# Local attention and the second projection of a vision-transformer block in one loop (Trainium2)

## The reference

```python
qkv = roll(xt @ w1.T + b1, (-2, -2))            # windows of 16 positions, 8 heads of 32
wei = einsum('bhijpe,bhijqe->bhijpq', Q, K) / scale + pos_emb[rel]   # masks in the last row and column
out = einsum('bhijpq,bhijqe->bhijpe', softmax(wei), V)
h = out.reshape(b, ht * wd, c) @ w2.T + b2      # the "hidden" product
qkv = layernorm(h) @ qkv_w + qkv_b              # q, k, v of the full attention
```

## Time and profile before

| | us |
|---|---|
| median of 3 runs | 6507.51 (6507.16 to 6508.6) |
| profiled execution | 6517.03, its span 6515.1 |
| window_attention and project_qkv, first matmul to last store | 105 to 1444.5 |
| PE busy over the span | 5921.2 (91%) |
| DVE, ACT, POOL busy | 4386.3 (67%), 3220.7 (49%), 4313.3 (66%) |

### The profile page before, as it was taken

The page is one execution under the profiler, slowest core; times in us unless marked ns, Lnnn a source line. Parts: engine busy times, 40 slices in busy tenths (PEclk is TensorE's granted clock), DMA queues, the critical chain, the costliest instruction groups (busy, mean ns, idle before and its releaser), DMA issues. The chain is left out here.

```text
span 6515.1 us, 122324 instructions
## 1 busy us (share of the span) xinstructions
PE 5921.2 (91%) x37810; PEld 3470.1 (53%) x37810; DVE 4386.3 (67%) x8624; ACT 3220.7 (49%) x6628; POOL 4313.3 (66%) x1449
## 2 busy tenths in 40 slices
PE   2777767769999999999999999999999999987899
PEld 2666645545555555555555555555555555533566
DVE  2666633337777778777777777777777777737540
ACT  1444421113666666666666666666666666651222
POOL 0222222234888888888888888888888888874453
PEclk9999989987999999999999999999999999997899
DMA  1111134442100110110110011011011000014432
GB/s 40 41 41 45 43 110 158 158 165 58 34 26 24 34 34 16 35 47 17 34 31 26 24 35 35 21 43 34 16 34 31 25 16 23 14 38 126 121 94 40
DMA packets 216264, 323.65 MB, mean 50 GB/s; under 512 B 42228, under 2 KB 181078, under 8 KB 212694
## 3 DMA queue, kind: packets, MB, share of 16 engines
q1 hardware_dynamic: 200670, 295.36, 15.8%
q0 software_dynamic: 12432, 19.38, 1.5%
q10 hardware_dynamic: 2664, 2.62, 0.2%
HBM read 179.54 MB, written 137.35 MB: 49 GB/s over the span
## 5 line engine op out<-in xcount | busy, mean ns | idle before, releaser
L1193 DVE TENSOR_REDUCE tops<-ps_m 128x1 f32<-128x448 f32 (+1 forms) x5600 | 3120.2, 618 | 906.6 <-PE ps_m L1096 856.5
L1169 ACT ACTIVATE prob<-ps_s 128x448 f32<-128x448 f32 (+1 forms) x5600 | 2613.6, 548 | 1749.4 <-PE ps_s L1032 1707.5
L1002 POOL TENSOR_TENSOR tile_sum<-prob 128x1792 f32<-128x1792 f32 x448 | 1803.5, 4026 | 658.3 <-ACT prob L1169 658.0
L1032 PE MATMUL ps_s<-queries,keys 97*128 97x448 f32 (+1 forms) x5600 | 2196.9, 397 | 15.3 <-ACT prob L1169 7.5
L1096 PE MATMUL ps_m<-keys,queries 96*128 96x448 f32 (+1 forms) x5600 | 2090.5, 380 | 35.7 <-DMA keys<-k_parts 20.6
L1002 POOL TENSOR_TENSOR tile_sum<-tile_sum,prob 128x1792 f32<-128x1792 f32 x448 | 1808.0, 4036 | 31.8
L1032 PEld LDWEIGHTS ps_s<-queries,keys 97*128 97x128 f32 (+1 forms) x5600 | 1041.4, 187 | 1156.3 <-ACT prob L1169 662.2
L1048 PE MATMUL ps_o<-prob,values 128*32 128x448 f32 x11200 | 1342.3, 551 | 3.0 <-ACT prob L1169 1.2
L1096 PEld LDWEIGHTS ps_m<-keys,queries 96*128 96x128 f32 (+1 forms) x5600 | 1061.3, 190 | 240.5 <-DVE tops L1193 84.5
L257 POOL TENSOR_TENSOR logit<-logit,top 112x896 f32<-112x896 f32 x112 | 188.6, 1684 | 559.5 <-DVE top L374 559.5
L1048 PEld LDWEIGHTS ps_o<-prob,values 128*32 128x32 f32 x11200 | 226.5, 108 | 379.5 <-issue 245.0
(11 more groups left out here) (174 smaller groups left out, 4361.7 us busy)
## 6 DMA issues: line engine op xcount, KB each, us to landing
queries<-q_parts SPq DMA_DIRECT2D x288, 160.0 KB, 3.3
keys<-k_parts SPq DMA_DIRECT2D x96, 392.0 KB, 6.9
xT<-in_x SPq DMA_DIRECT2D x56, 224.0 KB, 2.5
window_out<-oT SPq DMA_DIRECT2D x56, 224.0 KB, 2.0
aT<-window_out SPq DMA_DIRECT2D x56, 224.0 KB, 3.7
hidden<-h SPq DMA_DIRECT2D x28, 448.0 KB, 4.4
q_parts<-hi SPq DMA_DIRECT2D x56, 224.0 KB, 1.9
q_parts<-lo SPq DMA_DIRECT2D x56, 224.0 KB, 2.0
```

What stands on the lines that cost most here:

```text
L1002: nc.gpsimd.tensor_tensor(tile_sum[k % 2][:, :, :], left, prob[:, t % SLOTS, :, :], ALU.add).then_inc(summed, 1)
L1032: mm = nc.tensor.matmul(o[:, 0:CH], keys[x.u][:, j, at:at + k], queries[x.v][:, j, own:own + CH], start=True, stop=not last, skip_group_ch ...
L1169: nc.scalar.activation(prob[0:k, t % SLOTS, j, :], ps_s[0:k, score_bank(x.hm, i), 0:CH], ACT.Exp).then_inc(exp_done, 1)
L1193: nc.vector.tensor_reduce(tops[0:rows, j, r - blocks[0], c:c + 1], ps_m[0:rows, e % MB, 0:CH], AX.X, ALU.max).then_inc(m_used, 1)
```

## The change

The two blocks become one, windows_and_qkv. Its loop has one round for two units, and in round m the pieces of three things stand between each other on every engine: the units 2m and 2m+1 (`units`), the hidden product and the layer norm of chunk m-1 (`norm`), and the q, k and v projections of chunk m-2 (`project`). The first two rounds lack what has no input yet, and two rounds without units end the loop. The units' output oT stays on chip and is read by `hidden` directly; window_out, its stores and its loads are gone.

On-chip banks are shared: the hidden and projected rows go through the two banks of ps_q and the second bank of ps_t (`third`), with waits written out for each use. project_qk fills one bank with two jobs; the two halves of v of a unit share a bank and are copied out by one VectorE operation. The normalizing of rows moves from VectorE to ScalarE (norm_rows: four activations with scale rstd and bias off = -mean x rstd; `offset` computes off on VectorE). The constants of both parts are loaded before the loop, and every engine waits for all of them; the biases added to 112 x 512 tiles are loaded two copies wide, not four. In the helpers, `hidden` is two groups of eight records, `project_2` one column job, `project_v2` half of v, `turn_xn` half of the transposes. full_attention and gated_ffn are as before.

```diff
+def windows_and_qkv(nc, d):
...
+        def rounds(engine, one):
+            one(0, True, False, False)
+            one(1, True, True, False)
+            with engine.Fori(2, ROUNDS - 1) as m:
+                one(m, True, True, True)
+            one(ROUNDS - 1, True, True, True, last=True)
+            one(ROUNDS, False, True, True)
+            one(ROUNDS + 1, False, False, True)
...
+            def one(m, units, norm, project, last=False, last_row=0):
+                if units:
+                    pair(m, last_row)
+                    if not last:
+                        load(m, 0)
+                if project:
+                    parts(m - 2, 0)
+                if norm:
+                    sp.wait_ge(h_kept, ONE + 2 * (m - 1) + 2)
+                    sp.dma_start(d.h1[m - 1], h1[:, :, :]).then_inc(h_out, 16)
+                if units and not last:
...
+            def one(m, units, norm, project, last=False):
+                if units:
+                    shift(4 * m + 1, 1)
+                if project:
+                    low(m - 2, 0)
+                if norm:
+                    root(m - 1)
+                if project:
+                    low(m - 2, 1)
+                if units:
+                    shift(4 * m + 2, 0)
+                    shift(4 * m + 3, 1)
+                if project:
+                    low(m - 2, 2)
+                    low(m - 2, 3)
+                if units and not last:
...
+            def hidden(m, a, bank):
+                if a == 0:
+                    pe.wait_ge(normalized, ONE + 4 * (m + 1))
+                for r in range(2):
...
+            def one(m, units, norm, project, last=False):
+                n, before = 2 * m, m - 2
+                if units:
+                    scores(n, 0, 1)
+                if project:
+                    project_2(before, 0, third)
+                if units:
+                    if project:
+                        pe.wait_ge(xT_kept, ONE + CT * before + 1)
+                    else:
+                        pe.wait_ge(v_kept, ONE + n + 1)
+                    project_qk(n + 1, 1, 0, 0)
+                if norm:
+                    if project:
+                        pe.wait_ge(xT_kept, ONE + CT * before + 2)
+                    hidden(m - 1, 0, bank[1])
+                if units:
+                    pe.wait_ge(qk_kept, ONE + QK * (n + 1) + 2)
+                    project_qk(n + 1, 1, 1, 0)
+                    if project:
+                        pe.wait_ge(full_ready, ONE + QK * before + 1)
+                    turn(n, 0)
+                    if norm:
+                        pe.wait_ge(h_kept, ONE + 2 * (m - 1) + 1)
+                    project_v(n + 1, 1, 1)
+                    pe.wait_ge(t_kept, ONE + 2 * n + 1)
+                if norm:
+                    if not units:
+                        pe.wait_ge(full_ready, ONE + QK * before + 1)
+                    hidden(m - 1, 1, third)
+                if units:
+                    weigh(n, 0, 0)
+                    if norm:
+                        pe.wait_ge(h_kept, ONE + 2 * (m - 1) + 2)
+                    turn(n, 1)
+                if project:
+                    if units:
+                        pe.wait_ge(qk_kept, ONE + QK * (n + 1) + 4)
+                    project_2(before, 1, bank[0])
+                if units:
+                    scores(n + 1, 1, 0)
+                    weigh(n, 0, 1)
+                    n = n + 1
+                    scores(n, 1, 1)
+                if project:
+                    if not units:
+                        if norm:
+                            pe.wait_ge(h_kept, ONE + 2 * (m - 1) + 2)
+                        else:
+                            pe.wait_ge(full_ready, ONE + QK * before + 1)
+                    project_2(before, 2, third)
+                if units and not last:
+                    pe.wait_ge(v_kept, ONE + n + 1)
+                    project_qk(n + 1, 0, 0, 1)
+                if project:
+                    pe.wait_ge(full_ready, ONE + QK * before + 2)
+                    project_2(before, 3, bank[0])
+                if units:
+                    if not last:
+                        pe.wait_ge(qk_kept, ONE + QK * (n + 1) + 2)
+                        project_qk(n + 1, 0, 1, 1)
+                    if project:
+                        pe.wait_ge(full_ready, ONE + QK * before + 3)
+                    turn(n, 0)
+                    if not last:
+                        if project:
+                            pe.wait_ge(full_ready, ONE + QK * before + 4)
+                        project_v(n + 1, 0, 0)
+                    pe.wait_ge(t_kept, ONE + 2 * n + 1)
+                if project:
+                    if not units:
+                        pe.wait_ge(full_ready, ONE + QK * before + 3)
+                    project_v2(before, 0, third)
+                if units:
+                    weigh(n, 1, 0)
+                    if project:
+                        pe.wait_ge(v2_kept, ONE + 2 * before + 1)
+                    turn(n, 1)
+                if project:
+                    if units and not last:
+                        pe.wait_ge(qk_kept, ONE + QK * (n + 1) + 4)
+                    elif norm:
+                        pe.wait_ge(h_kept, ONE + 2 * (m - 1) + 1)
+                    project_v2(before, 1, bank[1])
+                if norm:
+                    if units and not last:
+                        pe.wait_ge(v_kept, ONE + n + 2)
+                    elif project:
+                        pe.wait_ge(full_ready, ONE + QK * before + 4)
+                    turn_xn(m - 1, 0, bank[0])
+                    if project:
+                        pe.wait_ge(v2_kept, ONE + 2 * before + 2)
+                    else:
+                        pe.wait_ge(qk_kept, ONE + QK * (n + 1) + 4)
+                    turn_xn(m - 1, 1, bank[1])
+                if units:
+                    if not last:
+                        scores(n + 1, 0, 0)
+                    weigh(n, 1, 1)
+            project_qk(0, 0, 0, 0)
...
+            def keep_h(m, a, bank):
+                if a == 0:
+                    dve.wait_ge(h_out, ONE + 16 * m)
+                    dve.wait_ge(xn_ready, ONE + NQ * m)
...
+            def one(m, units, norm, project, last=False):
+                n, before = 2 * m, m - 2
+                if units:
+                    logits(n, 0, 1)
+                if project:
+                    high(before, 0)
+                if norm:
+                    keep_h(m - 1, 0, bank[1])
+                if units:
+                    keep_v(n + 1, 1, 1)
+                if norm:
+                    keep_h(m - 1, 1, third)
+                if units:
+                    outputs(n, 0, 0)
+                if norm:
+                    moments(m - 1)
+                if project:
+                    high(before, 1)
+                if units:
+                    logits(n + 1, 1, 0)
+                    outputs(n, 0, 1)
+                    n = n + 1
+                    logits(n, 1, 1)
+                if norm:
+                    offset(m - 1)
+                if project:
+                    high(before, 2)
+                    high(before, 3)
+                if units and not last:
+                    keep_v(n + 1, 0, 0)
+                if project:
+                    keep_v2(before, 0, third)
+                if units:
+                    outputs(n, 1, 0)
+                if project:
+                    keep_v2(before, 1, bank[1])
+                if units:
+                    if not last:
+                        logits(n + 1, 0, 0)
+                    outputs(n, 1, 1)
...
+            def one(m, units, norm, project, last=False):
+                n, before = 2 * m, m - 2
+                if project:
+                    keep(before, 0, third)
+                if units:
+                    keep_qk(n + 1, 1, 0, 0)
+                    keep_qk(n + 1, 1, 1, 0)
+                    keep_t(n, 0)
+                    exps(n, 1)
+                    keep_sums(n, 0)
+                    keep_t(n, 1)
+                if project:
+                    keep(before, 1, bank[0])
+                if units:
+                    keep_sums(n, 1)
+                    exps(n + 1, 0)
+                    n = n + 1
+                if project:
+                    keep(before, 2, third)
+                if units and not last:
+                    keep_qk(n + 1, 0, 0, 1)
+                if project:
+                    keep(before, 3, bank[0])
+                if units:
+                    if not last:
+                        keep_qk(n + 1, 0, 1, 1)
+                    keep_t(n, 0)
+                if norm:
+                    norm_rows(m - 1)
+                if units:
+                    exps(n, 1)
+                    keep_sums(n, 0)
+                    keep_t(n, 1)
+                if norm:
+                    keep_xT(m - 1)
+                if units:
+                    keep_sums(n, 1)
```

(68 more changed lines are left out.)

484 lines of the change are left out of this document (142 added, 342 removed).

## The result

The changed kernel takes 6252.32 us (median of 4 runs, 6247.48 to 6258.19) against 6507.34 for the kernel before, beside it on the same chip: a ratio of 0.9609, 95% interval [0.9597, 0.9621]. That is 255 us less; 260 had been forecast, and the prediction of 6247.5 is 5 us off.

The account below looks back on a forecast made before the run. Bound: chains of waits between engines, no engine full. Start, rounds 0 and 1, 26 rounds of 37.5 us and tail sum to 1068 us, ending at 1184.5 against 1444.50: gain 260, 6507.5 - 260 = 6247.5 us, range 6185 to 6345.

Parts of the forecast that it names:

- the walk: One steady merged round stepped by hand over all engines: 33.0 us TensorE work plus 4.4 gaps, taken as 37.5.
- scores(B,1): TensorE's scores group for the round's second unit B (first is A), waiting for VectorE's logits(B,0): gap 2.0 us.
- the sums: TensorE's turn(A,1) and turn(B,1) each wait for ScalarE's copy of the sums: 0.75 us each.
- Rival (a): Merged loop: pieces fill no holes, chunk work merely lies beside today's pair; 40.7 us a round, 6331; chance 0.20.
- Rival (b): Merged loop: TensorE's gaps close because work runs ahead; 33.0 us a round, 6130.5; chance 0.10.
- The lock of GpSimd: VectorE operations beside GpSimd's nine a round: 0.13 us delay each, about 1.0 us more, mostly in VectorE's slack.
- the signs that the prediction had named: Stated as proof of error: TensorE waiting for full or qk, VectorE held by parts, VectorE operations longer beside GpSimd's.
- Rival (c): All four GpSimd lo subtractions a round stop VectorE in front of logits: 4.5 us, 6364.5; chance 0.08.
- Rival (d): Store waits come along, 10.6 us a chunk on VectorE in front of the units' logits: 6523; chance 0.04.
- step (4): DMA: window_out's transfers go, h1's landing is awaited a round later, both VectorE store waits go; late loads priced at nothing.
- round 1: The merged loop's second round, units and a hidden product without second-projection jobs: taken as 30.5 us.
- The clock: TensorE's clock, nearly always 2.4 GHz before; the merged round was said to lack holes that lower it; given nothing.

Follow-up runs that it names:

- the second stage alone: Kernel before, not merged: second stage's h1 store issued from ScalarE's queue, four buffers each of full, hi and lo; 6364.66 us, 0.9781.
- both orders together: Changed kernel, two reorderings: VectorE's logits(B,0) ahead of statistics and second cast; TensorE's scores and weigh(B,1) moved into its idle times; 6160.13 us, 0.9463.
- the run that filled the sums holes: Changed kernel, order only: scores between weigh(.,0) and turn(.,1), weigh(B,1) between turn_xn's halves, ScalarE's second xnT copy behind the sums copy; 6252.96 us, 0.9609.
- the run through memory: Changed kernel with the units' output stored to device memory and loaded back, the hidden product reading that copy; 6508.44 us, 1.0003.

## Why the prediction was right, step by step

**The round** was 37.46 us where the walk had 37.5, and by its parts. The holes sum to 4.06 (walked 4.4): before scores(B,1) 1.67 (2.0), the sums 0.76 and 0.83 (0.75 each), turn_xn 0.40 (0.45), scores(A,1) 0.40 (0.35). The rest, 33.4, had been 33.0. So the two errors, a third of a microsecond each, cancel, and that the sum is right to 0.04 us is luck; that each part came out within 0.4 us is not. The chain to scores(B,1), from the end of weigh(A,0), took 6.40 us where 6.45 was walked, and TensorE's cover for it 4.7 instead of 4.5. Rival (a), 40.7, is what the second stage alone gives, 26.1 + 14.7 = 40.8 apart: the interleaving did fill. Rival (b), 33.0, is nearly reached by both orders together (33.97), but only by moving steps on TensorE and VectorE, not in the order that was forecast. The walk's value lay less in the total than in the list of who waits for whom, from which the two orders of the faster kernels were read.

**The other engines** were as walked: 471.03, 328.12 and 237.08 us busy of 700 make 25.2, 17.6 and 12.7 us a round for VectorE, ScalarE and GpSimd (walked 25.6, 18 and 11.3 with one small operation). ScalarE's normalizing step, priced at 0.42 from the 128x224 row between bounds of nothing and 0.63, took 0.51:

```profile
627.39 2.06 ACT L738 ACTIVATE xn<-h,off,rstd 112x256 f32<-112x256 f32 x4
```

**The lock of GpSimd** was mis-sized in kind. It was priced at 0.13 a meeting; it is an exclusion that lasts until GpSimd's operation ends. The trace of before had this already, timeline of GpSimd:

```profile
408.69 1.68 POOL L257 TENSOR_TENSOR logit<-logit,top 112x896 f32<-112x896 f32 x1 [8.85 <-DVE top L374]
```

It ends at 410.37, 0.27 us after the pair of 0.59 us in the earlier trace rows began (410.10): the pair lost little because it met only the end. In the merged loop, timeline of GpSimd and of VectorE, two casts of one shape:

```profile
624.23 1.83 POOL L324 TENSOR_TENSOR logit<-logit,top 112x896 f32<-112x896 f32 x1 [2.52 <-DVE top L581]
```

```profile
624.14 0.39 DVE L637 CAST hi<-full 128x448 fp32r<-128x448 f32 x1
624.97 1.34 DVE L637 CAST hi<-full 128x448 fp32r<-128x448 f32 x1 [0.45 <-ACT full L731]
```

The second cast takes 1.34 us instead of 0.39, and ends 0.25 behind the shift (626.06). The Trainium skill, SBUF — State Buffer, section on the two separate sides of SBUF, states this exclusion for the whole instruction, and this trace and the 1.98 us above agree. One meeting does not. In the run with `lo` on VectorE, timeline of both:

```profile
600.99 1.21 POOL L330 TENSOR_TENSOR rstd<-veps,minus_half 112x4 f32<-112x4 f32 x1 [10.73 <-DVE veps L619]
601.37 0.63 DVE L632 TENSOR_TENSOR lo<-full,hi 128x448 fp32r<-128x448 f32 x1
```

Inside GpSimd's operation on 112x4 the same subtraction took its usual 0.63 us; why is open. The longer cast is one of the signs that the prediction had named for being wrong (VectorE's operations longer beside GpSimd's than these rows). It cost nothing because of its place: no TensorE step waits for that cast, and in the chain to scores(B,1) VectorE's steps have their usual times. Rival (c) had the right mechanism, without the path.

**The stores.** Rival (d) is refuted: no idle time of VectorE in the loop ends with a DMA, and the h1 wait is gone, as step (4) had it.

**The ends** were 4.1 us longer than the sum (1188.6 against 1184.5). The start was 116.87 (116.5; the prediction's own terms, 105.07 + 11, give 116.1), round 0 took 27.0 (26.3), round 1 took 186.70 - 153.22 = 33.5 where 30.5 was taken; the 26 rounds from there to 1159.41 took 972.7 (971), the tail 29.2 (31). The failed term is round 1: there TensorE lacks the second projection's jobs ahead of scores(B,1), which waits 2.20 us (two later holes take 1.29 and 1.69), and the products behind it are slow. TensorE's timeline:

```profile
170.93 0.90 PE L392 MATMUL ps_s<-qk 32*112 32x112 f32 x16 [2.20 <-DVE logit L576]
171.76 3.17 PE L371 MATMUL ps_q<-xT,w_qkv 128*128 128x224 f32 x8
```

**The clock** was given nothing, and in the steady loop of the change that was nearly right. But the reason, that the merged round lacks such holes, was thin: with a hole 0.6 us longer, though the others were shorter, the run that filled the sums holes lost 1.5 us a round. And the change itself lost 1.6 us in two of the loop's rounds, behind the same 1.67 us as in all others. TensorE's timeline in the second:

```profile
806.14 1.10 PE L392 MATMUL ps_s<-qk 32*112 32x112 f32 x16 [1.67 <-DVE logit L576]
807.17 2.91 PE L439 MATMUL ps_t<-xnT,w_qkv 128*128 128x448 f32 x4
```

## What to carry to other kernels

Walk one steady round over all engines before merging loops, and split the expected gain by its source: here 143 of 255 us were waits for stores and the clock lost behind them, to be had by a second queue and two more buffers each. When a hole is filled, ask what else hangs on the chain behind it; where a neighbour in another queue does, move the chain, and look at all holes together, since a fill can take its work from ahead of another hole. A hole has two prices, its length and the slower products behind it.

## What the runs showed of the hardware

TensorE's clock reacts to a small difference in idle time. With holes of 0.76, 1.67, 0.83, 0.40 and 0.40 us a round the granted clock from 300 to 1000 us was 1.00, its upper level of 2.4 GHz. With holes of 0.17, 2.26 and 0.24, less in sum, it was 0.95, and the groups behind the 2.26 ran mostly at the lower level, 1.2 GHz: the granted clock is 0.57 from 620.31 to 624.02 us, and a group took 2.84 us where 1.77 is usual. The length of the last hole does not decide alone. Behind a hole of 2.33 us, in the run with `lo` on VectorE, the four records took 2.48 us in one round and 1.77 in the next; behind 1.67 us they took 1.77 in the steady loop but for two rounds (2.94 and 2.91), and 2.96 in the run through memory, in whose round a hole of 5.06 had gone before. Which rule decides between them is left open.

VectorE and GpSimd exclude each other for some pairs of operations. Beside a shift of 112x896 a 128x448 cast took 1.34 us for 0.39 and a subtraction 1.98 for 0.62, ending 0.25 and 0.47 us behind the shift; the shift that met a running cast took 1.83 us instead of 1.68.
